# Moving a 46 KiB tile of matmul operands by 64 bytes in SBUF

## The reference

```python
# cross-attention of 256 tokens over 4096 context rows and themselves
q, k_new, v_new = ln(x) @ wq.T, ln(x) @ wk.T, ln(x) @ wv.T
scores = q @ concat([ctx, k_new]).T / sqrt(512)          # 256 x 4352
x = x + softmax(scores) @ concat([ctx, v_new]) @ wo.T
# causal latent attention, 16 heads, low-rank queries and keys, rotary part of 64
x = x + attention(ln(x), Wqa, Wqb, Wkva, Wkvb, Wo)
# experts: 32 routed (8 of them per token) and a shared one of twice the width
h = silu(ln(x) @ gate[e]) * (ln(x) @ up[e])              # 256 x 256 for each e
x = x + sum_e weight[:, e] * (h @ down[e])
```

## Time and profile before

| | |
|---|---|
| median of 3 runs | 533.22 us (532.43 to 533.89) |
| profiled execution, first to last instruction | 530.3 us (the page gives no other time of it) |
| TensorE busy | 520.7 us, 98%, 3454 matmuls |
| weight loads busy | 469.0 us, 88% |
| VectorE, ScalarE, GpSimd busy | 389.1, 304.3, 29.4 us |
| granted TensorE clock | 1.00 of full speed |
| DMA, mean share of 16 engines | 48% |

### The profile page before, as it was taken

How to read it: one execution, slowest core, us unless ns; L and a number is a source line. 1 busy time by engine, 2 the same in 40 slices (tenths; PEclk the granted TensorE clock), 3 DMA queues, 4 the chain that set the end, 5 groups by cost and what they waited for, 6 DMA issues and landing times.

```text
span 530.3 us, 9657 instructions
## 1 busy us (share of the span) xinstructions
PE 520.7 (98%) x3454; PEld 469.0 (88%) x3454; DVE 389.1 (73%) x616; ACT 304.3 (57%) x470; POOL 29.4 (6%) x48
## 2 busy tenths in 40 slices
PE   9999999999989999989999999999999999999997
PEld 7988888888669989879989999999999999999997
DVE  6777555557788988776987777768677776767675
ACT  5665587753476776637546465554646465554631
POOL 1000000000632131010000000000000000000000
PEclk9999999999999999999999999999999999999999
DMA  8775624455412232516355646464554646455521
GB/s 286 289 231 175 209 99 155 162 159 157 127 35 78 86 136 90 199 41 237 121 183 173 203 157 222 143 225 163 193 189 167 204 161 223 146 215 171 185 71 40
DMA packets 19459, 86.24 MB, mean 163 GB/s; under 512 B 2160, under 2 KB 2416, under 8 KB 19312
## 3 DMA queue, kind: packets, MB, share of 16 engines
q1 hardware_dynamic: 19440, 85.99, 47.9%
HBM read 85.46 MB, written 0.52 MB: 162 GB/s over the span
## 4 chain that ended last, share of the span: by engine, by line
PE 92%; DVE 5%; ACT 2%; issue 1%; POOL 0%; ACTq 0%; DVEq 0%; POOLq 0%
PE bank L936 33%; PE bank L429 16%; PE bank L433 16%; PE bank L432 16%; PE bank L437 2%; PE bank L501 1%; PE bank L438 1%; PE bank L439 1%; PE bank L573 1%; DVE w_lo L282 1%; PE bank L715 1%; PE bank L735 1%; PE bank L696 1%; ACT operands L305 1%; PE bank L455 1%
## 5 line engine op out<-in xcount | busy, mean ns | idle before, releaser
L277 ACT CAST w_hi<-raw 128x768 fp32r<-128x768 f32 (+3 forms) x158 | 158.9, 1040 | 96.6 <-PE bank L936 82.8
L282 DVE TENSOR_TENSOR w_lo<-raw,w_hi 128x1280 fp32r<-128x1280 f32 (+3 forms) x156 | 182.7, 1213 | 13.5 <-ACT w_hi L277 11.4
L429 PE MATMUL bank<-w_hi,operands 128*128 128x512 f32 (+1 forms) x322 | 126.1, 392 | 1.2 <-DVE operands L330 1.0
L433 PE MATMUL bank<-w_hi,operands 128*128 128x512 f32 (+1 forms) x322 | 124.0, 385 | 0.0
L432 PE MATMUL bank<-w_lo,operands 128*128 128x512 f32 (+1 forms) x322 | 123.8, 385 | 0.0
L936 PE MATMUL bank<-xt_hi,w_lo 128*128 128x256 f32 x512 | 108.6, 283 | 0.0
L936 PE MATMUL bank<-xt_hi,w_hi 128*128 128x256 f32 x512 | 108.4, 283 | 0.0
L936 PE MATMUL bank<-xt_lo,w_hi 128*128 128x256 f32 x512 | 108.3, 283 | 0.0
L936 PEld LDWEIGHTS bank<-xt_hi,w_hi 128*128 128x128 f32 x512 | 83.7, 190 | 2.6
L936 PEld LDWEIGHTS bank<-xt_hi,w_lo 128*128 128x128 f32 x512 | 81.7, 190 | 0.0
L936 PEld LDWEIGHTS bank<-xt_lo,w_hi 128*128 128x128 f32 x512 | 81.7, 190 | 0.0
(11 more groups left out here) (182 smaller groups left out, 565.4 us busy)
## 6 DMA issues: line engine op xcount, KB each, us to landing
raw<-w_exp_dram SPq DMA_DIRECT2D x34, 896.0 KB, 4.7
raw<-w_exp_dram SPq DMA_DIRECT2D x34, 640.0 KB, 5.6
raw<-ctx_t_dram SPq DMA_DIRECT2D x16, 512.0 KB, 4.6
raw<-ctx_n_dram SPq DMA_DIRECT2D x16, 512.0 KB, 4.1
raw<-w_mla_dram SPq DMA_DIRECT2D x8, 512.0 KB, 3.6
raw<-w_mla_dram SPq DMA_DIRECT2D x8, 448.0 KB, 3.9
raw<-wq_dram SPq DMA_DIRECT2D x4, 256.0 KB, 5.4
raw<-wk_dram SPq DMA_DIRECT2D x2, 512.0 KB, 7.3
```

The source lines that it names most:

```text
L277: act.copy(w_hi[:, t.slot, at:at + n], raw[:, t.slot, at:at + n]).then_inc(hi_split[k], 1)
L282: eng.tensor_tensor(w_lo[:, t.slot, at:at + n], raw[:, t.slot, at:at + n], w_hi[:, t.slot, at:at + n].bitcast(F32), ALU.subtract) \
L429: ins = pe.matmul(o, a[0], b[0], start=start, stop=False)
L433: return pe.matmul(o, a[1], b[0], start=False, stop=stop)
```

## The change

The two small tiles are asked for behind `operands` instead of ahead of it. `operands` then starts at 144384, which is 1128 times 128, and ends at 191488; `q_neg` and `q_root` lie at 191488 and 191520; `scores` stays at 191552. All other tiles and every instruction, wait and queue stay as they are, apart from the addresses.

```diff
         rope_raw = probs[:, :, :, :].rearrange("p a b n -> p (a b) n")
-        q_neg = sb("q_neg", [P, 2])
-        q_root = sb("q_root", [P, 2])
 
 
         operands = sb("operands", [P, 11776], F32R)
...
                                **dict(zip(names[1:], shape[1:])))
+
+        q_neg = sb("q_neg", [P, 2])
+        q_root = sb("q_root", [P, 2])
 
         q_hi, q_lo = op(0, NC, T), op(1024, NC, T)
```

## The result

The changed kernel takes 535.54 us (median of 4 runs, 534.87 to 536.22), the kernel before, run beside it, 533.27. The ratio is 1.0049, with a 95% interval of 1.0034 to 1.0065. The forecast was 534.0 us and no difference that shows. A difference shows, since the interval excludes 1; the time lies in the range that was given, but at the place of the third rival, 535.7 us, and not of the forecast.

A forecast was written before the change was run, and what follows sets the result against it. TensorE's pace was taken to bound the kernel. Five terms summed to +0.75 us, giving a 531.1 us span and, with 2.9 carried over, 534.0 us; 8-in-10 range 531.3 to 535.9, no difference that shows.

The forecast's parts named there:

- the third rival: Whole kernel: short 512-column runs never settle in time and pay 2 ns a matmul; 535.7 us, slower; chance 0.16.
- Term 1: Scores, one run of 192 matmuls: 9 intervals slower by 2 ns, 182 faster by 2 ns; -0.35 us.
- Term 2: Probabilities times values, 8 runs of 24: 9 intervals slower and 14 faster by 2 ns each; -0.1 us.
- Term 3: `down`, 33 runs of 12: 9 intervals slower and 3 faster by 2 ns, +12 ns a run; +0.4 us.
- term 4: Output projection and latent output, 120 matmuls in runs of 12 or fewer: ten times +12 ns; +0.1 us.
- Term 5: Queries, keys and values of 8 pairs, 144 matmuls of 256 columns: from 114 to 118 to 120 ns; +0.7 us.
- Never settles: Short runs, all but the scores, never reach 227 ns in time and pay 2 ns a matmul; 535.7 us; chance 0.16.
- No effect: Whole kernel: pace differences come from something else between stages, so moving the tile changes none; 533.2 us; chance 0.22.
- Settles at once: `down` settles within a matmul or two, all 906 512-column matmuls gain 2 ns; 531.4 to 532.1 us; chance 0.21.
- The signs that were named: Profile after: scores 227 ns late, `down` 2.75 to 2.77 us, 256-column matmuls 118 to 120, weight load 190 ns or more.

The follow-up runs named there:

- run 2: Changed kernel with 64 bytes of padding ahead of `operands`, putting it back at 144448, so only the two small tiles moved behind it; 532.66 us, ratio 0.9993.
- run 1: Changed kernel with 128 bytes of padding ahead of `operands`, so its start is at distance 0 from the weights; 532.65 us, ratio to the kernel before 0.9989.
- run 4: Changed kernel with the weights and all tiles between them and `rope_w` moved up 128 bytes, leaving `operands` at distance -256; 532.83 us, ratio 0.9996.
- run 5: Two tiles moved at once, `operands` 256 bytes above the weights and tokens 32 below, single execution; scores settle at 226.9 ns, total time not given.
- run 8: Tokens 64 bytes below the weights and `operands` at distance 0, both placings at once; 529.21 us, ratio to the kernel before 0.9928.
- run 7: Kernel before with the tokens `xt_hi` and `xt_lo` placed 64 bytes below the offset of the weights, `operands` left in place; 524.81 us, ratio 0.9843.
- run 12: Tokens 64 bytes below the weights and `operands` 96 above, single execution; 532.77 us.

## Why the prediction was right or wrong

**What bounds the kernel, and what is priced:** right. Only TensorE's pace moved the end; VectorE and ScalarE kept their durations within 2 ns, the small tiles cost nothing that shows (run 2), and no order was changed.

**The step that failed** is the definition of *alike*: that two operands are alike when both start at the same offset from a multiple of 128 bytes, and that the change makes `operands` alike with the weights. The span is 256 bytes (runs 1, 4 and 5), the weights lie 128 past a multiple of it, and the change took the distance from -64, a good place with 229 ns, to -128, a poor one with 232. The two stages from which 227 ns was read had distance 0 under either definition, so the rows did not separate 128 from 256; the addresses did, had I taken them modulo more than 128. That the time lies in the range is no merit of the mechanism: the range took in a rival with another ground.

**Terms 1 to 4** rest on runs that settle at 227, which none of them did. Terms 1 and 2 came out with the wrong sign: scores -0.35 predicted, +0.66 measured without the waits; values -0.1 and +0.65. Term 3 had the right sign and half the size: +0.4 and +0.75 in the experts. Output and 256-column matmuls together (terms 4 and 5): +0.8 and +0.68. The sum was +0.75 us, and 2.7 by the profile, 2.3 by the medians.

**Term 5** was right in size, 119 ns where 118 to 120 was said, and by luck: the pair is not alike but 128 bytes apart, and goes at 119 there as it does at 0 (run 1).

Run 1 is the change that the prediction priced, a pair at distance 0. Its windows of scores, values, latent attention and experts:

```profile
20.79:64.52 43.73, 43.73 (x194) 35.96 (x193) 31.89 (x36) 26.56 (x35) 0.00 (x0) 1.00 0.61 198
78.46:126.33 47.87, 47.87 (x239) 40.04 (x238) 29.00 (x33) 29.81 (x50) 0.00 (x0) 1.00 0.50 158
126.33:252.20 125.87, 120.51 (x888) 105.12 (x886) 102.96 (x256) 79.06 (x170) 27.59 (x40) 1.00 0.33 115
252.20:530.51 278.31, 275.33 (x1940) 258.92 (x1938) 205.07 (x256) 147.03 (x173) 0.00 (x0) 1.00 0.50 169
```

Against the kernel before that is -0.35, -0.14, +0.57 and -0.06 us: terms 1 and 2 as priced, 4 and 5 a little under the 0.8, and term 3 nothing in place of +0.4, since the slow start and the settled end of a `down` come to 229 together, as before.

**The rivals.** *Never settles* had the right end, 535.7 against 535.54, with 232 ns for the 231 that it was priced at; its ground, writers beside the run, was wrong, since run 1 settles beside the same ones. *No effect* is excluded by the interval and by the paces. Its ground was a rule of the Trainium skill ("TensorE: Matmul & The Clock Gate", Part 2: weight loads and moving operands are read through ports of their own). What the prediction drew from it, that the place of the operands could not show, does not hold here: with nothing but addresses changed, 512-column matmuls go at 227 to 234 ns and 256-column ones at 114 to 120. *Settles at once* needed pairs at distance 0, which the change did not make. With them `down` settles at once in run 8 (2.72 us) and not in run 1 (229.2 ns), and run 1's time differs from that of the kernel before by no more than the noise (0.9976 to 1.0002).

**The signs that were named** did half their work. The scores' pace, away from both 227 and 229, gave the failure away. `down` at 2.77 us and the 256-column matmuls at 119 stood as signs of the forecast and came true all the same; of the three signs of being wrong (the scores at 229, a pace of 220 or below, a VectorE or ScalarE group changed by 10 ns) none came. The mean weight load stayed at 188 ns and did not follow the pace.

**What stays open.** What makes the distance count, and why a pair of placings has two paces. I take it that the state in which a run is entered decides between them, since `gate_up` reads the same addresses in runs 7, 8 and 12, and in run 12 changes its pace within one execution; this is argued, no run set the entry by itself. In the projections of `q` and `k` it is not the other engines' writes to `operands`, which begin later; in the experts that was not tried. A pace of the table can so be one of several for its distance, those for 256 columns above all. Distances finer than 32 bytes were not tried, nor pieces of `w_hi` and `w_lo` at different offsets.

## What to carry to other kernels

Where TensorE is the bound and every matmul has a weight load of its own, the place of the two operands against each other is worth 1 to 5% of a stage: read the pace from start to start, and try moving one tile by some tens of bytes before touching the program. Alignment to a round number is no aim in itself; the fastest version here has the tokens 64 bytes off the weights, and the change that aligned a tile cost 0.5%. Try placings on the whole kernel, since the gain of one stage can change when another's operand is moved (runs 7 and 8).

## What the runs showed of the hardware that was not expected

A float32r matmul's pace with a weight load beside it changes with the distance between the two operands, modulo 256 bytes as far as tried (0, -256 and +256 agree): 227, 229, and 232 to 234 ns for 512 columns, 114, 117 to 118 and 120 ns for 256, at a granted clock of 1.00. The same distance below and above is not the same for 512 columns: 229 and 233 ns at 64 bytes in the scores, in values and in the projection of `v`. And one pair of placings can hold either of two paces for a whole run of 48, between executions of two programs (114.0 and 117.8 ns, runs 7 and 8) and within one execution (113.5 and 117.8, run 12).
